# Probabilities times values in a merged attention and expert stage: the values become the stationary operand

## The chip, the cores and the metric

One Trainium2 chip, one of its cores. The metric is the device time of one execution in microseconds, the median of three timed executions. One further execution was recorded by the hardware profiler, and all rows below come from it.

## The reference

A four-layer network on x of 32 batches x 128 rows x 128 columns; every sub-layer is added to x under a tanh gate. The change lies in one of two independent pieces of work which the kernel runs merged in one stage: the third layer's mixture of eight experts, and the fourth layer's attention, cut to this:

```python
x = x + tanh(g_ffn[2]) * L2_ffn(layernorm(x))       # 8 experts, top 2 of 8
# then, a batch of 128 rows at a time, 16 heads of 8 columns:
q, k = split(layernorm(x) @ WqT), split(ctx @ WkT)   # v = split(ctx)
scores = q @ k.T * 8 ** -0.5                         # 16 x 128 x 128
kth    = top_k(scores, 32)[..., -1:]                 # the 32nd largest of each row
p      = softmax(where(scores >= kth, scores, min))
x      = x + tanh(g_xattn[3]) * (p @ v)              # 128 x 128 a batch
```

## The kernel before

One program, written by hand for each engine with semaphores. The stage is `l3_attention`; a tile is one batch (128 rows), and there are 32.

Each engine runs a list of steps in the order in which `schedule` is given them; a pair `(step, behind)` runs `step` for tile `c - behind` in iteration `c`. So iteration c does the query projection and the scores of tile c+1, the row maxima and the cut-offs of tile c, the exponentials and masks of tile c-1, the product with the values for tile c-2, and the division and addition for tile c-3. Experts (`hide`, `gelu`, `output`, `take_y`, `add_experts`) run four tiles ahead in the same lists.

The steps that the change and the prediction touch, for one tile:

- `cutoffs` (VectorE, L2746): 112 instructions, MAX8 and MATCH_REPLACE8, which find the 32nd largest score of each row of each head.
- `negate_max` (GpSimd, L2391) writes `nm` for half of the heads; `exps` n (ScalarE, L2624) then makes the exponentials of heads 4n to 4n+3; `mask` (GpSimd, L2404) zeroes those under the cut-off. For tile 31 the second half is done by VectorE (`negate_last`, `mask_last`).
- `turn_probs` n (TensorE, L2511): four 128x128 transposes into `p_ps`; `take_p` n (ScalarE, L2607) copies these 128x512 into `pT`.
- `apply` n (TensorE, L2518): for each of four heads one matmul with the turned probabilities (128x128) as weights and nine moving columns, the head's eight value columns and a column of ones whose product is the row sum. One matmul in fp32 is two pairs of LDWEIGHTS and MATMUL in the records, so `apply` n is eight pairs.
- `divide` (VectorE, L2766) waits for `av_mm`, the semaphore of the four `apply`, takes the reciprocal of the row sums and multiplies; `add_attention` (GpSimd, L2419) adds to x. `divide` of tile c waits for `x_done` of tile c-1, and `apply` 0 of tile c for `o_ready`, the end of `divide` of tile c-1, since there is one bank `ov_ps`.

On TensorE an iteration is: output 0, hide 0 and 1, output 1, turn_probs 0, turn_rows, hide 2 and 3, apply 0, turn_probs 1, queries, hide 4 and 5, apply 1, turn_probs 2, scores 0, hide 6 and 7, bias_rows, apply 2, turn_probs 3, turn_weights, apply 3, scores 2. Each `apply` n waits for `p_ready` of its `take_p`.

From iteration 32 on, engines that were given `draining` use that list instead. ScalarE's is take_p 0 to 3 (of tile c-2) and then exps 0 to 3 (of tile c-1). VectorE's is divide, negate_last, mask_last; GpSimd's is negate_max 0, mask 0, add_attention. TensorE has none.

After the stage comes a barrier (L2365) and the normalisation `n3f`, whose first instruction is BATCH_NORM_STATS2 at L292.

Of the kernel before, what the change touches and what calls it, by code (L numbers as in the profile page):

```python
# [10 lines left out]
ACT = mybir.ActivationFunctionType  # L11
# [3 lines left out]
P = 128  # L15
# [5 lines left out]
BANK = 512  # L21
# [25 lines left out]
def per_row(ap, n):  # L47

    return ap.unsqueeze(2).to_broadcast([ap.shape[0], ap.shape[1], n])
# [2184 lines left out]
def l3_attention(nc, k):  # L2234
# [4 lines left out]
    H, DA, ROUNDS = 16, 8, 4  # L2239
    Q4, NQ = 4, 4  # L2240
# [3 lines left out]
    AHEAD = 4  # L2244
# [8 lines left out]
    with ExitStack() as ctx:  # L2253
        s = Space(nc, ctx, "l3a", k)
# [2 lines left out]
        w1, w2, b1, bias8, router_bias = wf.w1, wf.w2, wf.b1, wf.bias8, wf.router_bias  # L2257
        two = range(2)
        v_raw = [s.sb(f"v_raw{i}", [P, D]) for i in two]
        v = [s.sb(f"v{i}", [P, H, DA + 1]) for i in range(4)]  # L2260
        qT, kT = s.sb("qT", [P, P]), [s.sb(f"kT{i}", [P, Q4, P]) for i in two]
        score = [s.sb(f"score{i}", [P, H, P]) for i in range(4)]
        work = s.sb("work", [P, H, P])
# [4 lines left out]
        pT = [s.sb(f"pT{i}", [P, Q4, P]) for i in two]  # L2268
# [15 lines left out]
        def spare(tile, start, *shape):  # L2284
            flat = tile[:, :, :].rearrange("p h s -> p (h s)")[:, start:start + int(np.prod(shape))]
            names = "abc"[:len(shape)]
            return flat if len(shape) == 1 else flat.rearrange(f"p ({' '.join(names)}) -> p {' '.join(names)}",
                                                               **dict(zip(names, shape)))
        NE, LQ = NB * E, 2 * NB
        p, rest, eq = (spare(score[3], i * NE, NB, E) for i in range(3))  # L2290
# [8 lines left out]
        ov_ps, p_ps, o2_ps, misc_ps = (s.ps(n, [P, BANK]) for n in ("o", "p", "l2o", "misc"))  # L2299
# [1 line left out]
        h_ps = [s.ps(f"l2h{i}", [P, BANK]) for i in two]  # L2301
        q_ps = s_ps[1][:, 0:P]
        prefix_ps, total_ps, early_ps = p_ps, ov_ps, s_ps[1]
        o_ps = ov_ps[:, 0:H * (DA + 1)].rearrange("p (h d) -> p h d", h=H)
        k_loaded, v_loaded = ([s.sem(f"{n}_loaded{i}") for i in two] for n in "kv")
        (filled, v_ready, q_mm, q_ready, s_mm, s_ready, found, nm_ready, probs_done, compared,
         masked, p_mm, p_ready, av_mm, inv_ready, o_ready, x_done) = (s.sem(n) for n in (
# [11 lines left out]
        def wait(eng, sem, q, per_element, value):  # L2319

            n = q * int(BODY * per_element) + value
            if not isinstance(q, int) or n >= 1:
                eng.wait_ge(sem, n)
# [30 lines left out]
        def in_group(step, at):  # L2354

            return lambda q, u: step(q, u // GT) if u % GT == at else None
# [4 lines left out]
        def for_part(step, n):  # L2361

            return lambda q, c: step(q, c, n)

        with nc.Block() as block:  # L2365
# [17 lines left out]
            def _(pool):  # L2383
# [1 line left out]
                pool.wait_ge(carry_made, 1)  # L2385
                pool.memset(carry[:, :, 0:1], 0.0).then_inc(carry_made, 1)
                for t in v:
                    pool.memset(t[:, :, :], 1.0).then_inc(filled, 1)
                pool.wait_ge(filled, 4)

                def negate_max(q, c, half):  # L2391
# [65 lines left out]
                def norm_scale(q, g):  # L2457
                    n = NORM_STEPS * g

                    def done(i):  # L2460
# [26 lines left out]
                         draining=[(for_part(negate_max, 0), 1), (for_part(mask, 0), 1), (add_attention, 3)])  # L2487

            @block.tensor
            def _(pe):  # L2490
# [27 lines left out]
                def apply(q, c, n):  # L2518
                    wait(pe, p_ready, q, NQ, NQ * c + n + 1)
                    if n == 0:  # L2520
                        wait(pe, v_ready, q, 1, c + 1)
                        wait(pe, o_ready, q, 1, c)
                    for i in range(Q4):
                        h = Q4 * n + i
                        ins = pe.matmul(o_ps[:, h, :], pT[n % 2][:, i, :], v[c % 4][:, h, :], start=True, stop=True)  # L2525
                    ins.then_inc(av_mm, 1)

                def hide(q, u, at):
                    x, i = at // 2, at % 2
                    wait(pe, act_done, q, 2 * EX, 2 * EX * u + at - 1)  # L2530
                    for n in two:
                        ins = pe.matmul(h_ps[i][:, n * WIDE:(n + 1) * WIDE], w1[:, expert(u, x), 2 * i + n, :],  # L2532
                                        k.cols[:, ds(group(q, u) * WIDE, WIDE)], start=True, stop=True)
                    ins.then_inc(h_mm, 1)
# [46 lines left out]
                for at in range(2 * EX):  # L2581
# [9 lines left out]
                              (for_part(scores, 0), -1), (for_part(hide, 6), -AHEAD), (for_part(hide, 7), -AHEAD),  # L2591
                              (in_group(bias_rows, 1), -AHEAD),
                              (for_part(apply, 2), 2), (for_part(turn_probs, 3), 2), (in_group(turn_weights, 0), -AHEAD),
                              (for_part(apply, 3), 2), (for_part(scores, 2), -1)], first=2 - AHEAD)

            @block.scalar
            def _(act):
# [9 lines left out]
                def take_p(q, c, n):  # L2607
                    wait(act, p_mm, q, NQ, NQ * c + n + 1)
                    wait(act, av_mm, q, NQ, NQ * c + n - 1)
                    act.activation(pT[n % 2][:, :, :], p_ps[:, :].rearrange("p (h s) -> p h s", h=Q4), ACT.Copy  # L2610
                                   ).then_inc(p_ready, 1)

                def take_y(q, u, x):
                    wait(act, o_mm, q, PARTS, PARTS * u + x + 1)
                    wait(act, x_added, q, ADDS, ADDS * (u - 1) + 2 * (x + 1))
                    if u % GT == 0:
                        wait(act, w_staged, q, GROUP, u // GT + 1)
                    for n in range(2 * GT):
                        e = expert(u, 2 * x + n // GT)
                        ins = act.activation(y[x][:, n, :], output_bank(u, x)[:, n * D:(n + 1) * D], ACT.Copy,  # L2620
                                             scale=w_stage[u // GT % 2][:, n % GT, e:e + 1])
                    ins.then_inc(y_ready, 1)
# [53 lines left out]
                for u in two:  # L2676
                    for at in range(2 * EX):
# [11 lines left out]
                               (take_queries, -1), (for_part(gelu, 4), -AHEAD), (for_part(gelu, 5), -AHEAD),  # L2689
                               (for_part(take_p, 2), 2), (for_part(take_scores, 0), -1), (for_part(gelu, 6), -AHEAD),  # L2690
                               (for_part(gelu, 7), -AHEAD), (in_group(take_bias, 1), -AHEAD),
                               (for_part(take_p, 3), 2), (in_group(take_weights, 0), -AHEAD), (for_part(take_scores, 2), -1)], first=2 - AHEAD,
                         draining=[*((for_part(take_p, n), 2) for n in range(NQ)), *((for_part(exps, n), 1) for n in range(NQ))])

            @block.vector
            def _(dve):
# [67 lines left out]
                            n += 1  # L2764

                def divide(q, c):  # L2766
                    wait(dve, av_mm, q, NQ, NQ * (c + 1))
                    wait(dve, x_done, q, 1, c)
                    dve.reciprocal(inv[:, :], o_ps[:, :, DA:DA + 1].rearrange("p h o -> p (h o)")).then_inc(inv_ready, 1)
                    wait(dve, inv_ready, q, 1, c + 1)  # L2770
                    dve.tensor_tensor(o_norm[:, :, :], o_ps[:, :, 0:DA], per_row(inv[:, :], DA), ALU.mult
                                      ).then_inc(o_ready, 1)
# [15 lines left out]
                def mask_last(q, c):  # L2788
# [3 lines left out]
                    for h in range(H // 2, H):  # L2792
# [4 lines left out]
                        if h % Q4 == Q4 - 1:  # L2797
# [3 lines left out]
                         draining=[(divide, 3), (negate_last, 1), (mask_last, 2)])  # L2801
# [265 lines left out]
def program(nc, d, out, first=0, last=99):  # L3067

    with ExitStack() as ctx:
# [37 lines left out]
            lambda: l2_cross(nc, k),  # L3107
            lambda: (normalise_measured(nc, k, "n2f", keep_rows=True, gate_w=k.gates_w[:, 2, :], logits=k.logits),
                     l3_attention(nc, k)),
            lambda: l3_block(nc, k),  # L3110
        ]
# [101 lines left out]
```

## Time and profile before

| | us |
|---|---|
| median of three timed executions | 3101.04 |
| lowest and highest of them | 3099.99, 3103.3 |
| the profiled execution's own time | 3106.62 |
| its span, first to last instruction | 3104.8 |
| busy in the span: PE, DVE, ACT, POOL | 2850.7, 2030.3, 1820.0, 1427.0 |

PE is TensorE's matmuls, PEld its weight loads, which overlap them, DVE VectorE, ACT ScalarE, POOL GpSimd. The mean granted clock of TensorE over the span was 0.924 of full speed. The ends of matmuls are modelled, so a distance from start to start says more than a busy time.

### The profile page before, as it was taken

The numbers are of one execution on the slowest core, as the hardware profiler recorded it, in microseconds if no ns is written. First come the engines' busy times: TensorE is split into PE (matmuls) and PEld (weight loads), VectorE is DVE, ScalarE is ACT, GpSimd is POOL, SyncE is SP. The second block draws the span as 40 slices with busy tenths as digits, with TensorE's granted clock in tenths as the row PEclk, the third lists the DMA queues.
The fourth block names the chain that finished last, engine by engine and source line by source line (L and its number), as shares of the span: only waits on it lengthen the run. The fifth ranks groups of instructions, "written<-read, shape, count | busy, mean of one in ns | idle before, by whom it ended". The sixth has DMA issues, their size and how long they took to land. (4 is left out here: it accounts for less than half of the span.)

```text
span 3104.8 us, 70254 instructions
## 1 busy us (share of the span) xinstructions
PE 2850.7 (92%) x21784; PEld 2265.4 (73%) x21784; DVE 2030.3 (65%) x7995; ACT 1820.0 (59%) x5314; POOL 1427.0 (46%) x1744
## 2 busy tenths in 40 slices
PE   7999979987998989999999998999999996597999
PEld 6888854433775778888888777888888874486676
DVE  4444536764653456666666459999999999486433
ACT  5777734443553356666666567788888873353333
POOL 2122117762542434444444248788888876452000
PEclk9999979987998989999999899899999985597999
DMA  3000024433763311111111000000000000001000
GB/s 114 6 5 6 5 53 85 82 82 112 260 235 95 126 49 54 54 54 54 54 54 54 16 10 14 14 13 13 13 13 13 13 14 32 2 18 36 7 10 10
DMA packets 99460, 151.81 MB, mean 49 GB/s; under 512 B 11312, under 2 KB 39488, under 8 KB 98752
## 3 DMA queue, kind: packets, MB, share of 16 engines
q1 hardware_dynamic: 99296, 149.96, 16.5%
q8 instruction: 62, 1.02, 0.1%
q14 instruction: 102, 0.84, 0.1%
HBM read 103.33 MB, written 46.47 MB: 48 GB/s over the span
## 5 line engine op out<-in xcount | busy, mean ns | idle before, releaser
L1899 POOL TENSOR_TENSOR l2a_probs<-l2a_probs,l2a_inv 128x1024 f32<-128x1024 f32 x128 | 242.3, 1893 | 370.5 <-DVE l2a_inv L2065 370.5
L2010 ACT ACTIVATE l2a_probs<-l2a_s_ps,l2a_nm 128x256 f32<-128x256 f32 x512 | 236.1, 472 | 200.0 <-DVE l2a_nm L2041 200.0
L2760 DVE MAX8 l3a_top<-l3a_work 128x8 f32<-128x128 f32 x1536 | 314.1, 276 | 0.0
L2544 PEld LDWEIGHTS l3a_l2o_ps<-net_arena 128*128 128x128 f32 x2016 | 276.6, 222 | 39.0 <-issue 34.9
L2411 POOL TENSOR_SCALAR l3a_above<-l3a_score,l3a_top 128x128 f32<-128x128 f32 x504 | 294.1, 601 | 16.3 <-POOL l3a_probs L2416 7.2
L2544 PE MATMUL l3a_l2o_ps<-net_arena 128*128 128x128 f32 x2016 | 283.4, 308 | 10.6 <-ACT net_l1f_gate L2620 10.6
L2762 DVE MATCH_REPLACE8 l3a_work<-l3a_top,l3a_work 128x128 f32<-128x128 f32 x1024 | 268.8, 274 | 0.0
L2532 PE MATMUL l3a_l2h_ps<-net_cols,net_arena 128*128 (+1 forms) x1024 | 250.9, 388 | 12.9 <-ACT net_arena L2652 11.2
L2532 PEld LDWEIGHTS l3a_l2h_ps<-net_cols,net_arena 128*128 128x128 f32 x1024 | 184.9, 191 | 65.8 <-ACT net_arena L2652 24.5
L721 ACT ACTIVATE l0a_probs<-l0a_score_ps,l0a_nm 128x128 f32<-128x128 f32 x512 | 179.6, 382 | 73.6 <-DVE l0a_nm L770 73.6
L2652 ACT ACTIVATE net_arena<-l3a_l2h_ps,net_l2f_b 128x256 f32<-128x256 f32 x512 | 210.0, 492 | 16.6 <-PE l3a_l2h_ps L2532 13.7
L2525 PEld LDWEIGHTS l3a_o_ps<-l3a_v,l3a_pT 128*128 128x128 f32 x1024 | 148.6, 217 | 73.6 <-ACT l3a_pT L2610 50.2
L755 POOL TENSOR_TENSOR l0a_v<-l0a_v,l0a_inv 128x1024 f32<-128x1024 f32 x32 | 60.9, 1902 | 300.4 <-DVE l0a_inv L794 300.4
L2525 PE MATMUL l3a_o_ps<-l3a_v,l3a_pT 128*128 128x9 f32 x1024 | 148.2, 272 | 49.7 <-ACT l3a_pT L2610 36.5
L2416 POOL TENSOR_TENSOR l3a_probs<-l3a_probs,l3a_above 128x512 f32<-128x512 f32 x126 | 160.2, 1272 | 47.1 <-ACT l3a_probs L2630 37.7
L2041 DVE TENSOR_REDUCE l2a_nm<-l2a_s_ps 128x2 f32<-128x512 f32 x256 | 159.0, 683 | 29.7 <-PE l2a_s_ps L1922 29.6
L2224 DVE SCALAR_TENSOR_TENSOR net_x<-l3f_o_ps,net_weight,net_x 128x128 f32 (+1 forms) x256 | 72.1, 344 | 139.9 <-PE l3f_o_ps L2141 139.5
L770 DVE TENSOR_REDUCE l0a_nm<-l0a_score_ps 128x4 f32<-128x512 f32 x128 | 82.1, 683 | 124.3 <-PE l0a_score_ps L681 124.3
L2630 ACT ACTIVATE l3a_probs<-l3a_score,l3a_nm 128x128 f32<-128x128 f32 x512 | 156.2, 396 | 8.9 <-POOL l3a_nm L2395 8.6
L2176 ACT ACTIVATE l3f_hidden<-l3f_h_ps 128x512 f32<-128x512 f32 x128 | 76.3, 597 | 145.0 <-PE l3f_h_ps L2132 145.0
L1973 PE MATMUL l2a_side_ps<-net_ident,l2a_probs 128*128 128x128 f32 x1024 | 153.4, 280 | 1.0 <-POOL l2a_probs L1899 0.7
L2141 PEld LDWEIGHTS l3f_o_ps<-net_arena,l3f_hidden 128*128 128x128 f32 x1024 | 124.2, 192 | 29.7 <-issue 18.2
(522 smaller groups left out, 7209.1 us busy)
## 6 DMA issues: line engine op xcount, KB each, us to landing
kv_ahead<-l1a_kept SPq DMA_DIRECT2D x128, 256.0 KB, 2.7
l0f_code<-code_rows SPq DMA_DIRECT2D x32, 512.0 KB, 11.5
l2a_kT<-kv_ahead SPq DMA_DIRECT2D x64, 256.0 KB, 2.6
l2a_v<-kv_ahead SPq DMA_DIRECT2D x64, 256.0 KB, 2.6
l1a_shift<-neg_top SPq DMA_DIRECT2D x16, 512.0 KB, 5.0
l1f_chosen<-mask_code SPq DMA_DIRECT2D x64, 128.0 KB, 3.1
keys_ahead<-l1f_keys_kept SPq DMA_DIRECT2D x32, 256.0 KB, 3.3
l3a_kT<-keys_ahead SPq DMA_DIRECT2D x32, 256.0 KB, 2.7
```

Of the source, the lines that this page charges most:

```text
L721: act.activation(probs[c % 2][:, h, :], score[g][:, i * P:(i + 1) * P], ACT.Exp, bias=nm[:, h:h + 1], accum_out=sums[c % 2][:, h:h + 1]).t ...
L1899: pool.tensor_tensor(p[:, :, :], p[:, :, :], per_row(inv[c % 2][a][:, :, :].rearrange("p i o -> p (i o)"), KV), ALU.mult).then_inc(scaled, 1)
L2010: act.activation(probs[c % 2][a][:, 2 * i + odd, :], s_ps[a][odd][:, i * KV:(i + 1) * KV], ACT.Exp, bias=nm[c % 2][a][:, i, odd:odd + 1], ...
L2041: dve.tensor_reduce(nm[c % 2][a][:, :, odd:odd + 1].rearrange("p i o -> p (i o)"), s_ps[a][odd][:, :].rearrange("p (i s) -> p i s", i=2), ...
L2411: ins = pool.tensor_scalar(above[:, i, :], score[c % 4][:, h, :], top[c % 2][:, ROUNDS - 1, h, 7:8], None, ALU.is_ge)
L2416: pool.tensor_tensor(probs[c % 2][:, hs, :], probs[c % 2][:, hs, :], above[:, :, :], ALU.mult).then_inc(masked, 1)
L2525: ins = pe.matmul(o_ps[:, h, :], pT[n % 2][:, i, :], v[c % 4][:, h, :], start=True, stop=True)
L2532: ins = pe.matmul(h_ps[i][:, n * WIDE:(n + 1) * WIDE], w1[:, expert(u, x), 2 * i + n, :], k.cols[:, ds(group(q, u) * WIDE, WIDE)], start=T ...
L2544: ins = pe.matmul(output_bank(u, x)[:, at:at + D], hidden[2 * x + n][:, i, j * P:(j + 1) * P], w2[:, expert(u, 2 * x + n), i, :], start=(i ...
L2652: ins = act.activation(hidden[x][:, 2 * i + n, :], h_ps[i][:, n * WIDE:(n + 1) * WIDE], ACT.Gelu, bias=b1[:, e, 2 * i + n:2 * i + n + 1])
L2760: ins = dve.max(t[:, step // 2, h, :], src)
L2762: ins = dve.match_replace(work[:, h, :], t[:, step // 2, h, :], src, LOWEST)
```

## The change

`apply` swaps the operands. The values of a head, widened from 9 to 32 columns (eight values, a one, 23 zeros), are the weights, and the head's turned probabilities are the 128 moving columns. The product of head 4n+i lands turned, in partitions 32i to 32i+31 of `ov_ps` and columns 128n to 128n+127. A new ScalarE step `take_o` copies the whole bank (128x512) to `oT`, and a new TensorE step `turn_out` makes four 128x128 transposes back into `ov_ps`; `divide` now waits for these. GpSimd fills four wider `v` tiles with zeros and then writes their columns of ones. ScalarE's draining list gets another order.

```diff
-        v = [s.sb(f"v{i}", [P, H, DA + 1]) for i in range(4)]
+        WV = 32
+        v = [s.sb(f"v{i}", [P, H, WV]) for i in range(4)]
+        oT = s.sb("oT", [P, BANK])
...
-        o_ps = ov_ps[:, 0:H * (DA + 1)].rearrange("p (h d) -> p h d", h=H)
+        o_ps = ov_ps[:, :].rearrange("p (h d) -> p h d", h=H)
+        v_blank, o_taken, o_turned = s.sem("v_blank"), s.sem("o_taken"), s.sem("o_turned")
...
                 for t in v:
-                    pool.memset(t[:, :, :], 1.0).then_inc(filled, 1)
+                    pool.memset(t[:, :, :], 0.0).then_inc(v_blank, 1)
+                for i, t in enumerate(v):
+                    pool.wait_ge(v_blank, i + 1)
+                    pool.memset(t[:, :, DA:DA + 1], 1.0).then_inc(filled, 1)
...
                         h = Q4 * n + i
-                        ins = pe.matmul(o_ps[:, h, :], pT[n % 2][:, i, :], v[c % 4][:, h, :], start=True, stop=True)
+                        ins = pe.matmul(ov_ps[WV * i:WV * i + WV, n * P:(n + 1) * P], v[c % 4][:, h, :], pT[n % 2][:, i, :],
+                                        start=True, stop=True)
                     ins.then_inc(av_mm, 1)
+
+                def turn_out(q, c):
+                    wait(pe, o_taken, q, 1, c + 1)
+                    for n in range(NQ):
+                        ins = pe.transpose(ov_ps[:, n * P:(n + 1) * P], oT[:, n * P:(n + 1) * P], k.ident[:, :])
+                    ins.then_inc(o_turned, 1)
...
-                              (for_part(apply, 3), 2), (for_part(scores, 2), -1)], first=2 - AHEAD)
+                              (for_part(apply, 3), 2), (for_part(scores, 2), -1), (turn_out, 2)], first=2 - AHEAD)
...
+                def take_o(q, c):
+                    wait(act, av_mm, q, NQ, NQ * (c + 1))
+                    wait(act, o_turned, q, 1, c)
+                    act.activation(oT[:, :], ov_ps[:, :], ACT.Copy).then_inc(o_taken, 1)
...
-                               (for_part(take_p, 3), 2), (in_group(take_weights, 0), -AHEAD), (for_part(take_scores, 2), -1)], first=2 - AHEAD,
-                         draining=[*((for_part(take_p, n), 2) for n in range(NQ)), *((for_part(exps, n), 1) for n in range(NQ))])
+                               (for_part(take_p, 3), 2), (in_group(take_weights, 0), -AHEAD), (take_o, 2), (for_part(take_scores, 2), -1)], first=2 - AHEAD,
+                         draining=[(for_part(take_p, 0), 2), (for_part(exps, 0), 1), (for_part(exps, 1), 1), (for_part(take_p, 1), 2),
+                                   (for_part(take_p, 2), 2), (for_part(take_p, 3), 2), (take_o, 2), (for_part(exps, 2), 1),
+                                   (for_part(exps, 3), 1)])
...
                 def divide(q, c):
-                    wait(dve, av_mm, q, NQ, NQ * (c + 1))
+                    wait(dve, o_turned, q, 1, c + 1)
```

## Rows read from the trace of the kernel before

**Rows 1.** Busy by window, with instruction counts, granted clock, DMA share and rate.

```profile
core 0: us, PE busy (x) PEld busy (x) DVE busy (x) ACT busy (x) POOL busy (x), PEclk, DMA share, GB/s
...
1975.00:2070.00 95.00, 92.00 (x595) 80.07 (x594) 94.90 (x610) 79.87 (x206) 77.89 (x131) 0.93 0.05 15
...
2638.00:2670.00 32.00, 21.73 (x92) 18.79 (x92) 4.19 (x17) 8.72 (x23) 5.76 (x8) 0.50 0.00 1
```

**Rows 2.** Timeline at tile 11's division: start, length, instruction, idle time before it.

```profile
2176.95 1.06 PE L2525 MATMUL l3a_o_ps<-l3a_v,l3a_pT 128*128 128x9 f32 x8 [0.69 <-ACT l3a_pT L2610]
...
2177.94 1.13 PE L2508 MATMUL l3a_s_ps<-l3a_kT,l3a_qT 32*128 32x512 f32 x4
...
2178.10 0.24 DVE L2769 RECIPROCAL l3a_inv<-l3a_o_ps 128x16 f32<-128x16 f32 x1
...
2179.10 1.08 ACT L2642 ACTIVATE l3a_score<-l3a_s_ps 128x512 f32<-128x512 f32 x2 [2.20 <-PE l3a_s_ps L2508]
```

**Rows 3.** Timeline at tile 0's division.

```profile
1892.44 1.06 PE L2525 MATMUL l3a_o_ps<-l3a_v,l3a_pT 128*128 128x9 f32 x8 [0.47 <-ACT l3a_pT L2610]
...
1896.99 0.23 DVE L2769 RECIPROCAL l3a_inv<-l3a_o_ps 128x16 f32<-128x16 f32 x1
```

**Rows 4.** Busy by window on both sides of the end of one iteration.

```profile
2175.00:2179.00 4.00, 3.31 (x24) 2.29 (x24) 3.97 (x26) 0.90 (x3) 3.05 (x7) 1.00 0.00 0
2179.00:2182.00 3.00, 3.00 (x19) 3.00 (x18) 3.00 (x22) 2.87 (x5) 2.42 (x5) 0.62 0.43 109
```

**Rows 5.** Timeline of TensorE at full clock in this stage, iteration's end.

```profile
2199.57 0.96 PE L2525 MATMUL l3a_o_ps<-l3a_v,l3a_pT 128*128 128x9 f32 x8
2200.38 0.63 PE L2515 MATMUL l3a_p_ps<-net_ident,l3a_probs 128*128 128x128 f32 x4
2200.85 0.38 PE L2553 MATMUL l3a_misc_ps<-net_ident,l3a_l2w_stage 128*8 128x128 f32 x2
```

**Rows 6.** Timeline of TensorE in a later attention stage (weights 128x32).

```profile
2749.72 0.39 PE L2998 MATMUL l3b_s_ps<-net_l3b_proj,l3b_aoT 128*128 128x128 f32 x2
2750.03 0.92 PE L2985 MATMUL l3b_out_ps<-l3b_v,l3b_pT 128*32 128x36 f32 x32
2750.89 0.50 PE L2967 MATMUL l3b_s_ps<-l3b_kT,l3b_qT 32*32 32x128 f32 x32
```

**Rows 7.** Timeline of TensorE in an earlier attention stage (weights 128x64).

```profile
1322.78 1.97 PE L1938 MATMUL l2a_av_ps<-l2a_pT,l2a_v 128*64 128x128 f32 x32
1324.67 0.60 PE L1949 MATMUL l2a_side_ps<-net_cols,net_arena 128*128 x3
```

**Rows 8.** Timeline of the stage's end, tiles 30 and 31.

```profile
2628.87 0.24 POOL L2395 TENSOR_SCALAR l3a_nm<-l3a_top 128x8 f32<-128x8 f32 x1
...
2629.64 0.60 ACT L2610 ACTIVATE l3a_pT<-l3a_p_ps 128x512 f32<-128x512 f32 x1 [2.91 <-PE l3a_p_ps L2515]
...
2638.22 0.24 DVE L2769 RECIPROCAL l3a_inv<-l3a_o_ps 128x16 f32<-128x16 f32 x1
...
2638.93 1.85 PE L2525 MATMUL l3a_o_ps<-l3a_v,l3a_pT 128*128 128x9 f32 x8 [9.33 <-DVE l3a_o_norm L2771]
...
2640.64 1.09 PE L2515 MATMUL l3a_p_ps<-net_ident,l3a_probs 128*128 128x128 f32 x4
2641.77 0.60 ACT L2610 ACTIVATE l3a_pT<-l3a_p_ps 128x512 f32<-128x512 f32 x1 [11.53 <-PE l3a_p_ps L2515]
...
2649.27 4.77 ACT L2630 ACTIVATE l3a_probs<-l3a_score,l3a_nm 128x128 f32<-128x128 f32 x16
...
2656.31 0.26 DVE L2769 RECIPROCAL l3a_inv<-l3a_o_ps 128x16 f32<-128x16 f32 x1 [17.45 <-POOL net_x L2422]
...
2657.04 1.85 PE L2525 MATMUL l3a_o_ps<-l3a_v,l3a_pT 128*128 128x9 f32 x8 [3.92 <-DVE l3a_o_norm L2771]
...
2669.44 0.26 DVE L2769 RECIPROCAL l3a_inv<-l3a_o_ps 128x16 f32<-128x16 f32 x1 [10.26 <-PE l3a_o_ps L2525]
```

**Rows 9.** Two GpSimd lines: durations min/median/max, first and last start.

```profile
L2388 POOL MEMSET l3a_v<- x4: 217/218/218, 1757.0 to 1757.4; 128x144 f32 x4
...
L2401 POOL TENSOR_SCALAR l3a_v<-l3a_v_raw,net_tg x32: 601/618/624, 1806.1 to 2588.0; 128x128 f32<-128x128 f32 x32
```

## The prediction

> **What bounds the kernel now.** I read the page first. TensorE is the busiest engine over the whole span, but the change touches one stage, so its own windows decide. Over 95 us in the middle of the stage VectorE is busy for 94.90 and TensorE for 92.00 [rows 1]. The timeline tells which of the two sets the pace. Tile 0 is divided at 1896.99, tile 11 at 2178.10 and tile 29 at 2638.22 [rows 2, 3, 8]: 25.56 us a tile over the first eleven and 25.56 over all 29, which is VectorE's unbroken row of cut-offs. TensorE is close behind. At tile 0 its last `apply` began 4.55 us before the division, at tile 11 only 1.15 [rows 2, 3]; as that `apply` lasts 1.06, its results were there 0.1 us before VectorE wanted them. TensorE has used up its lead but does not yet hold VectorE back.
>
> Behind tile 29's division VectorE has no cut-offs left, and the order changes: the stage lasts 31.2 us more, until the division of tile 31 at 2669.44, with TensorE at half its clock (0.50, which is 1.2 GHz) [rows 1, 8]. This tail is a chain through TensorE and ScalarE. `apply` 0 of tile 30 starts at 2638.93, released by VectorE. Then for each n comes a cycle: 1.71 us of `apply`, 1.09 of four transposes, 0.60 of `take_p`, and gaps of 0.04 and 0.05, together 3.5 us [rows 8]. The exponentials of tile 31 stand behind all four `take_p` in ScalarE's list and start at 2649.27, though their row maxima, for the first half, were ready at 2629.11 [rows 8]. The mask and the addition follow, so tile 30 is divided only at 2656.31, after 17.45 us of waiting for GpSimd; three more cycles end at 2669.44 [rows 8].
>
> **The change, part by part.**
>
> *The groups of `apply` at full clock.* Eight pairs take 0.81 us from their start to that of the next group [rows 5], and 0.99 in front of the scores [rows 2]; I take 0.85. The new form, 32 columns of weights and 128 moving, is in no row. Its nearest relatives bound it. Weights of 128x32 with 36 moving: 32 instructions in 0.86 us, 27 ns each [rows 6]. Weights of 128x64 with 128 moving: 32 in 1.89 us, 59 ns each [rows 7]; a full-width instruction with 128 moving columns needs about 0.12 (0.47 us for four transposes [rows 5]), so two column halves run side by side. Four quarters should need 27 to 30 ns each, at best 0.22 us a group; without any overlap 8 x 0.112 = 0.9. Entering the form costs a little: two instructions before it take 0.31 us instead of the 0.22 of a steady row [rows 6], so 0.09, and I allow the same for leaving. I take 0.45 us a group, since halves already overlap, and keep 0.4 and 1.1 as ends. Four groups save 4 x 0.40 = 1.6 us of TensorE a tile. The Trainium skill, TensorEngine Tiling, section Key Properties, says that a change of tiling mode drains TensorE; the trace agrees in kind and prices it at that 0.09 us.
>
> *The four transposes of `turn_out`*: 0.47 us at full clock [rows 5], 1.09 at half [rows 8]. Net, TensorE does 1.1 us less a tile.
>
> *`take_o`*: a 128x512 copy like `take_p`, 0.60 us [rows 8]. In the steady part it starts when `apply` 3 ends, about when the scores start at 2177.94. `take_scores`, next behind it in ScalarE's list, waits until 2179.10 anyway, after 2.20 us of idle time [rows 2]: hidden. If TensorE answered that much sooner, it would cost ScalarE 0.6 us of 25.6. `turn_out` sits behind the scores, 1.06 us long, so it finds `oT` ready. What queues behind it is `output` 0, whose turn is 0.5 us later.
>
> *The later signal to `divide`*: it comes behind the scores and transposes, 1.06 + 0.5 + 0.2 us of latency, 1.7 us later than `av_mm`. Taken alone this would make VectorE wait, since it has 0.1 us. But VectorE's pace stays 25.56 while TensorE's falls to about 24.4, so TensorE goes ahead 1.1 us a tile, until ScalarE waits for the row maxima. From a lead of 3.5 us at tile 0 less 1.7, it never touches zero. Steady part: no gain and no loss, the cover being VectorE's cut-offs. Were that cover gone, the gain would be 1.1 us x 29 = 32 us.
>
> *GpSimd's fills*: 128x144 takes 0.22 us [rows 9]; 128x512 is 3.6 times that at most, so 3.2 us for four and under 1 for the small ones, from 1757 on; the first values are written at 1806.1 [rows 9]. Nothing. Writing and reading at a stride of 32 instead of 9 elements: same counts, nothing.
>
> *The tail*, where it counts. At half clock a group's start-to-start time was 1.71, 0.214 a pair [rows 8]. New: 8 x 0.054 for four quarters plus 0.2 for entering and leaving, 0.65. The cycle becomes 3.5 - 1.06 = 2.42. With the new list, ScalarE makes exps 0 and 1 of tile 31 right behind `take_p` 0 of tile 30 at 2630.2, ready by 2633 (0.30 each: 4.77 for 16), under VectorE's cut-offs; the masks of the first half are done before 2638. Now the chain:
> - `apply` 0 of tile 30: 2638.93, not moved. Three cycles: `apply` 3 starts at 2646.2, ends 0.85 later, 2647.05.
> - `take_o` 0.65 with its gap: 2647.7. `turn_out` 1.14: 2648.8. `divide` and multiplication 0.6: 2649.4.
> - exps 2 and 3 behind `take_o`: eight x 0.30, 2650.1. `mask_last` follows head by head, in time for `turn_probs` 2. `take_p` 0 of tile 31: 2650.7.
> - `apply` 0 at 2650.75, three cycles, 2658.0; its end 2658.85; `take_o` 2659.5; `turn_out` 2660.65; `divide` there.
>
> So 2660.65 against 2669.44: 8.8 us. With the overlap of halves only (0.107 a pair), the cycle is 2.83 and the gain 5.4; with none it is 0.2; with free mode changes 10.2. I take 8.8.
>
> Sum: the profiled execution 3106.62 - 8.8 = 3097.8. That execution ran 5.6 above the median; on the median, 3101.04 - 8.8 = 3092.2.
>
> **The rivals.**
>
> 1. *The quarters run one behind another* (the change doesn't do what it says). Each group costs 8 x 0.112 + 0.2 = 1.1 us instead of 0.85; with the transposes TensorE needs 1.5 us more a tile. It already paces VectorE within 0.1 us, so every tile from about the third waits: 27 x 1.5 plus 1.7 for the later signal, less the lead of 3.5, 39 us; the tail gives 0.2. Time 3140. It decides from 0.74 us a group on (0.85 less a quarter of 0.47). For it: no row shows this form. Against: the 59 ns of the halves and the 27 of the quarters. The Trainium skill, TensorE: Matmul & The Clock Gate, Part 3, The mechanism, says that a weight load overlaps a running matmul only if its row group is another; all quarters here use all 128 rows, so by that rule this rival happens. The trace disagrees at 27 and 59 ns. Chance 0.09.
>
> 2. *The clock takes the steady part's slack.* The granted clock is 1.00 from 2175 to 2179, while TensorE has gaps (3.31 busy of 4.00), and 0.62 in the next three microseconds, where it is fully busy [rows 4]: each iteration pays some 1.7 us after its thin end. With less TensorE work the thin stretches grow. A second such fall in each iteration would put TensorE at 24.4 + 1.7 = 26.1 us, 0.5 over VectorE: 14.5 us in 29 tiles, less the lead of 1.8, 13. But it falls only after gaps, and gaps vanish when TensorE is late, so I expect part of it: 0 to 13 us against the tail's 8.8, time 3092 to 3105, most likely 3099. Chance 0.15.
>
> 3. *The tail gains less*, because entering and leaving the form costs more at half clock, or cycles hang on something hidden until now (GpSimd's mask, `mask_last`): 4 to 6 us, 3096. Chance 0.08.
>
> 4. *More*: the clock falls less often, in the tail or behind it, where falls last 3 us and more each: 3084 to 3088. Chance 0.05.
>
> **How the numbers follow.** Forecast 0.63; the rivals 0.09, 0.15, 0.08, 0.05. A measurement of this kernel can tell about 0.2%, 6.2 us: faster ends at 3094.8, slower begins at 3107.2. The forecast's own spread is 3089 to 3096, a little of it inside the bound. Faster: 0.57 of the forecast, 0.02 of rival 2, 0.02 of rival 3, 0.04 of rival 4, 0.65. Slower: rival 1 and 0.05 for the tail of rival 2, 0.14. Same: 0.21. The range 3085 to 3104 holds all but rival 1 and the ends of 2 and 4.
>
> **What would show it.** Right: L2525 as 128*32 with 128 moving, 27 to 40 ns each at full clock; tiles 0 to 29 still 25.56 us apart; tile 29's division at 2638; `turn_out` ending 2 us or more before the division in the steady part; the exponentials of tile 31 starting near 2630; divisions at 2649 and 2660.6. Wrong: DVE L2769 waiting in the middle of the stage for `turn_out` (rivals 1 and 2, told apart by the pace of L2525 and by the granted clock), or cycles above 2.6 us in the tail (rival 3).

## The result, and the profile after

| | before | after |
|---|---|---|
| median of eight timed executions each, us | 3104.94 | 3093.59 |
| lowest and highest | 3099.99, 3110.65 | 3086.55, 3098.28 |
| the profiled execution's own time | 3106.62 | 3095.26 |
| its span | 3104.8 | 3093.5 |
| busy in the span: PE, DVE, ACT | 2850.7, 2030.3, 1820.0 | 2775.3, 2030.8, 1839.8 |
| mean granted clock | 0.924 | 0.934 |

The medians are 11.35 us apart, where 8.8 were forecast. The ratio is 0.9961, 95% interval 0.9947 to 0.9974, which is 8 to 16.5 us. Twice more against the kernel before it came to 0.995 (0.9934 to 0.9967) and 0.996 (0.9946 to 0.9974).

The windows of the changed kernel beside [rows 1], the columns as there:

```profile
1975.00:2070.00 95.00, 86.09 (x615) 66.29 (x615) 94.90 (x606) 81.59 (x205) 77.70 (x129) 0.96 0.04 12
2638.00:2660.00 22.00, 13.14 (x90) 7.26 (x88) 4.35 (x17) 7.59 (x17) 0.94 (x2) 0.50 0.00 1
```

In mid-stage VectorE is as busy as before, 94.90 of 95 us, and still the pace. TensorE issues 20 instructions more and is busy for 5.9 us less, at a clock of 0.96 instead of 0.93. The groups of `apply`, now L2531, at full clock (timeline of TensorE, beside [rows 5]):

```profile
2037.49 0.42 PE L2531 MATMUL l3a_o_ps<-l3a_pT,l3a_v 128*32 128x128 f32 x8
2037.85 0.66 PE L2521 MATMUL l3a_p_ps<-net_ident,l3a_probs 128*128 128x128 f32 x4
```

From the start of a group to that of the next it takes 0.36 us, where the old form had 0.81. The same group through two narrow windows, its first four instructions and its last four:

```profile
2037.49 0.32 PE L2531 MATMUL l3a_o_ps<-l3a_pT,l3a_v 128*32 128x128 f32 x4
2037.63 0.29 PE L2531 MATMUL l3a_o_ps<-l3a_pT,l3a_v 128*32 128x128 f32 x4
```

A single one is recorded with 0.297 us in the first four and 0.272 in the last, so four starts lie within some 0.02 us: about 7 ns from one to the next. Then comes a step of 0.11 us, and the next four again start 7 ns apart. The eight go in two waves of four, one head in each quarter, and the second wave starts 0.13 us after the first. From its last start to the next group pass 0.20 us. A wave by itself costs 0.11 us, so two make 0.22; the other 0.14 of the 0.36 is entering and leaving the form, for which the prediction had allowed 0.18.

The end of the stage (timeline, beside [rows 8]):

```profile
2626.75 2.44 ACT L2648 ACTIVATE l3a_probs<-l3a_score,l3a_nm 128x128 f32<-128x128 f32 x8 [1.73 <-POOL l3a_nm L2401]
...
2635.83 0.24 DVE L2789 RECIPROCAL l3a_inv<-l3a_o_ps 128x16 f32<-128x16 f32 x1
...
2636.55 0.65 PE L2531 MATMUL l3a_o_ps<-l3a_pT,l3a_v 128*32 128x128 f32 x8 [12.17 <-DVE l3a_o_norm L2791]
2637.13 1.12 PE L2521 MATMUL l3a_p_ps<-net_ident,l3a_probs 128*128 128x128 f32 x4
2638.29 0.60 ACT L2623 ACTIVATE l3a_pT<-l3a_p_ps 128x512 f32<-128x512 f32 x1 [9.09 <-PE l3a_p_ps L2521]
2638.93 0.65 PE L2531 MATMUL l3a_o_ps<-l3a_pT,l3a_v 128*32 128x128 f32 x8 [0.69 <-ACT l3a_pT L2623]
...
2643.71 0.65 PE L2531 MATMUL l3a_o_ps<-l3a_pT,l3a_v 128*32 128x128 f32 x8 [0.69 <-ACT l3a_pT L2623]
2644.43 0.60 ACT L2629 ACTIVATE l3a_oT<-l3a_o_ps 128x512 f32<-128x512 f32 x1 [0.77 <-PE l3a_o_ps L2531]
2644.92 2.43 ACT L2648 ACTIVATE l3a_probs<-l3a_score,l3a_nm 128x128 f32<-128x128 f32 x8
2645.08 1.12 PE L2538 MATMUL l3a_o_ps<-net_ident,l3a_oT 128*128 128x128 f32 x4 [0.72 <-ACT l3a_oT L2629]
...
2646.23 0.26 DVE L2789 RECIPROCAL l3a_inv<-l3a_o_ps 128x16 f32<-128x16 f32 x1 [9.75 <-PE l3a_o_ps L2538]
...
2657.57 0.26 DVE L2789 RECIPROCAL l3a_inv<-l3a_o_ps 128x16 f32<-128x16 f32 x1 [8.46 <-PE l3a_o_ps L2538]
```

One cycle is 2638.93 - 2636.55 = 2.38 us (3.5 before). Tile 30 is divided 10.40 us after tile 29 (18.09 before), tile 31 21.74 us after it (31.22 before): the tail is 9.5 us shorter. From tile 0's division (1894.79) to tile 29's 741.0 us pass, as before (741.2), and behind the stage 435.9 (435.4). So in these two executions tiles 0 to 31 give 9.7 of the 11.3 us between the spans; tile 0's division itself comes 2.2 us earlier (1896.99 and 1894.79), and 0.5 is lost again behind the stage. Over the profiled executions below that have VectorE's work unchanged, tile 0's division lies anywhere from 1882 to 1897 us, so from here on the stage is measured from there: "steady" is tile 0's division to tile 29's, "tail" tile 29's to tile 31's, both from the timelines.

### The profile page after: what moved, and what is told of

It reads as the page before. It is cut to its first block and busy times, and to the rows that moved or that the text cites. A ratio compares the mean times of both kernels' runs of the same rounds, so it can differ in the third digit from the quotient of the medians.

```text
span 3093.5 us, 70580 instructions
## 1 busy us (share of the span) xinstructions
PE 2775.3 (90%) x21912; PEld 2135.8 (69%) x21912; DVE 2030.8 (66%) x7995; ACT 1839.8 (59%) x5346; POOL 1428.5 (46%) x1748
## 3 DMA queue, kind: packets, MB, share of 16 engines
q1 hardware_dynamic: 99296, 149.96, 16.5%
## 5 line engine op out<-in xcount | busy, mean ns | idle before, releaser
L2557 PE MATMUL l3a_l2o_ps<-net_arena 128*128 128x128 f32 x2016 | 264.9, 295 | 40.6 <-ACT net_l1f_gate L2638 40.0
L2557 PEld LDWEIGHTS l3a_l2o_ps<-net_arena 128*128 128x128 f32 x2016 | 258.0, 211 | 52.8 <-ACT net_l1f_gate L2638 35.7
L2670 ACT ACTIVATE net_arena<-l3a_l2h_ps,net_l2f_b 128x256 f32<-128x256 f32 x512 | 210.3, 492 | 16.2 <-PE l3a_l2h_ps L2545 14.7
L2054 DVE COPY l2a_pT<-l2a_side_ps 128x512 f32<-128x512 f32 x128 | 88.6, 692 | 77.3 <-PE l2a_side_ps L1973 77.3
L1973 PEld LDWEIGHTS l2a_side_ps<-net_ident,l2a_probs 128*128 128x128 f32 x1024 | 111.8, 141 | 34.8 <-DVE l2a_pT L2054 14.1
## 6 DMA issues: line engine op xcount, KB each, us to landing
l0f_code<-code_rows SPq DMA_DIRECT2D x32, 512.0 KB, 11.3
```

The source lines that it names most:

```text
L1973: ins = pe.transpose(side[j][:, h * P:(h + 1) * P], probs[c % 2][a][:, h, j * P:(j + 1) * P], k.ident[:, :])
L2557: ins = pe.matmul(output_bank(u, x)[:, at:at + D], hidden[2 * x + n][:, i, j * P:(j + 1) * P], w2[:, expert(u, 2 * x + n), i, :], start=(i ...
L2670: ins = act.activation(hidden[x][:, 2 * i + n, :], h_ps[i][:, n * WIDE:(n + 1) * WIDE], ACT.Gelu, bias=b1[:, e, 2 * i + n:2 * i + n + 1])
```

## The experiments

The first theory: the gain is the tail alone, about half of it from the form and half from ScalarE's new order, and the steady part is VectorE's and gives nothing. The rivals: the steady part gives something too, or the clock does.

| kernel | steady, us | tail, us | median | ratio, interval |
|---|---|---|---|---|
| before, profiled | 741.2 | 31.2 | | |
| before, three more profiles | 743.7, 750.0, 744.3 | 31.2 each | 3104.41, 3113.64, 3108.49 (one execution each) | |
| changed | 741.0 | 21.7 | 3093.59 | 0.9961, 0.9947 to 0.9974 |
| changed, again | 741.1 | 21.7 | 3090.30 | 0.9950, 0.9934 to 0.9967 |
| changed, third | 741.1 | 21.7 | 3094.36 | 0.9960, 0.9946 to 0.9974 |
| order alone | 750.0 | 27.1 | 3101.32 | 0.9979, 0.9967 to 0.9991 |
| form alone | 741.1 | 26.5 | 3097.53 | 0.9972, 0.9962 to 0.9983 |
| one quarter | 749.2 | 27.8 | 3108.16 | 1.0004, 0.9991 to 1.0017 |
| before, less VectorE | 741.2 | 32.1 | 3086.45 | 0.9932, 0.9908 to 0.9956 |
| changed, less VectorE | 667.7 | 21.7 | 3007.45 | 0.9686, 0.9656 to 0.9716 |
| warm before the tail | 741.1 | 21.1 | 3091.28 | 0.9954, 0.9936 to 0.9971 |
| two banks | 741.1 | 13.2 | 3085.24 | 0.9934, 0.9920 to 0.9948 |

The first row of the changed kernel is the result above, against 3104.94 us. Each other ratio is against executions of the kernel before in the same series: 3107.36 us for the first four below, 3108.17 for less VectorE and for warm, 3107.12 for two banks and the third run of the changed kernel.

**The changed kernel again.**

> The changed kernel once more, as the yardstick of this call. If the gain comes from the stage's tail, the time from tile 29's division to tile 31's is again 21.8 us (31.2 before) and the total about 9 to 12 us under before.

It came to 0.995, 17.1 us by the medians and so more than the 9 to 12 expected, with steady part and tail as in its first profile.

**The order alone.** The kernel before, but for ScalarE's draining list:

```diff
-                         draining=[*((for_part(take_p, n), 2) for n in range(NQ)), *((for_part(exps, n), 1) for n in range(NQ))])
+                         draining=[(for_part(take_p, 0), 2), (for_part(exps, 0), 1), (for_part(exps, 1), 1), (for_part(take_p, 1), 2),
+                                   (for_part(take_p, 2), 2), (for_part(take_p, 3), 2), (for_part(exps, 2), 1),
+                                   (for_part(exps, 3), 1)])
```

> The kernel before with ScalarE's new draining order alone. Theory: tail divisions hang on the chain through TensorE and on the exponentials; with exps 0 and 1 of tile 31 moved ahead, tile 30 is divided right behind its apply 3 (13.1 us after tile 29 instead of 18.1) and take_p 0 of tile 31 waits for exps 2 and 3, so tile 31 is divided 26.6 us after tile 29 instead of 31.2: 4.6 us gained. Rival, all gain is the new order: 9.5 us gained. Rival, all gain is the new product form: 0.

The tail is 4.1 us shorter (4.6 expected), and tile 30 is divided 13.1 us after tile 29, as expected. Not expected was the steady part, 8.7 us longer than in the profile of before, though no step in it was touched. VectorE's only wait in this kernel between 1900 and 2600 us (who waited for whom: us in total, times, longest), and its window beside [rows 1]:

```profile
DVE l3a_inv L2771 <- PE l3a_o_ps L2525: 8.3, 5, 2.9
```

```profile
1975.00:2070.00 95.00, 91.34 (x552) 77.33 (x552) 90.97 (x579) 73.96 (x188) 74.38 (x127) 0.89 0.04 11
```

The divisions wait five times for the last `apply`; the clock stands at 0.89. That called for more profiles of the kernel before, below.

**The form alone.** The changed kernel with the old order at the end:

```diff
-                         draining=[(for_part(take_p, 0), 2), (for_part(exps, 0), 1), (for_part(exps, 1), 1), (for_part(take_p, 1), 2),
-                                   (for_part(take_p, 2), 2), (for_part(take_p, 3), 2), (take_o, 2), (for_part(exps, 2), 1),
-                                   (for_part(exps, 3), 1)])
+                         draining=[*((for_part(take_p, n), 2) for n in range(NQ)), (take_o, 2),
+                                   *((for_part(exps, n), 1) for n in range(NQ))])
```

> The changed kernel with the old draining order (take_p 0 to 3, take_o, then exps 0 to 3). Theory: cycles of 2.39 us, but the exponentials of tile 31 start only behind take_p 3 or take_o of tile 30, about 9 us after tile 29's division, and mask, addition and division follow 7 us later; tile 31 is divided 26.6 us after tile 29, 4.6 us gained. Rival, all gain is the order: 0 or a loss of 1 to 2 us from take_o and turn_out. Rival, all gain is the form: 9.5 us.

The tail is 4.7 us shorter (4.6 expected). The exponentials of tile 31 again stand behind the whole of tile 30 (a row of its timeline):

```profile
2632.55 4.77 ACT L2648 ACTIVATE l3a_probs<-l3a_score,l3a_nm 128x128 f32<-128x128 f32 x16
```

4.1 and 4.7 make 8.8 of the 9.5 us that both give together. The 0.7 that is left has no run of its own; with the form alone `take_o` of tile 30 stands ahead of these exponentials, too, and that may be it.

In time the form alone gives 9.8 us (interval 5.3 to 11.8) and the order alone 6.0 (2.8 to 10.3). The form's interval lies above the 4.7 us of its tail, so in the timed executions, too, the form gives something beyond the tail.

**All four heads of a group in one quarter.** Same instructions, same work, but the heads that follow one another use the same 32 columns (`divide` reads its bank in the order that this gives; not shown):

```diff
-                        ins = pe.matmul(ov_ps[WV * i:WV * i + WV, n * P:(n + 1) * P], v[c % 4][:, h, :], pT[n % 2][:, i, :],
+                        ins = pe.matmul(ov_ps[WV * n:WV * n + WV, i * P:(i + 1) * P], v[c % 4][:, h, :], pT[n % 2][:, i, :],
```

> The changed kernel, with the four heads of a group all in the same 32-column quarter (group n in quarter n, head i in column block i) instead of one in each; same instructions, same result. Theory, the quarters run side by side: without it a group takes 0.9 to 1.1 us at full clock, 1.7 to 1.9 at half, TensorE again has no slack and VectorE waits for it: 20 to 40 us slower than before, the tail's cycles 3.5 us. Rival, a load of 32 columns alone makes the group short: group 0.5 us or less as in the changed kernel and the time the same as that one's.

This makes rival 1 true. Its timeline and its windows:

```profile
2173.42 1.06 PE L2531 MATMUL l3a_o_ps<-l3a_pT,l3a_v 128*32 128x128 f32 x8
2174.41 0.66 PE L2521 MATMUL l3a_p_ps<-net_ident,l3a_probs 128*128 128x128 f32 x4
```

```profile
1975.00:2070.00 95.00, 89.58 (x590) 70.87 (x589) 94.79 (x605) 80.34 (x204) 77.68 (x130) 1.00 0.04 12
```

(1.06 - 0.27) / 7 = 0.113 us a step, where a whole wave of four costs that in the other layout, and a group is 0.99 us, not 0.36. That the quarters run side by side is hereby shown, and it is what the form's speed is made of. In the tail a cycle is 3.64 us (3.5 expected).

The time was missed: 3108.16 us against 3107.36, no slower, where 20 to 40 us were expected. The steady part grew by 8 us only. Against the old form TensorE has 4 x (0.99 - 0.85) + 0.47 = 1.0 us a tile more to do, which would be 30 us in 29 tiles at the clock of before. But the second row has a granted clock of 1.00, and the next experiment says what that is worth. Once its lead is gone, from tile 9 to tile 25, this kernel takes 26.0 us a tile, 0.4 over VectorE's 25.56.

**The cover removed.** In both kernels VectorE's cut-offs take three rounds of MAX8 instead of four, so they keep the 24 largest scores, not 32; the rest is untouched:

```diff
-    H, DA, ROUNDS = 16, 8, 4
+    H, DA, ROUNDS = 16, 8, 3
```

> The kernel before with three rounds of cut-offs instead of four (the 24 largest scores are kept, not 32), so that VectorE needs about 18.5 us a tile and no longer sets the pace. Theory: TensorE with ScalarE then sets it, at 24 to 25.5 us a tile. Together with its partner (the same cut in the changed kernel) it measures what TensorE's work is worth when nothing covers it: predicted 1.1 us a tile, some 32 us over the stage, plus the tail's 9.5. Rival: the steady part is bound elsewhere (GpSimd, 20.7 us busy a tile, or ScalarE), and the two differ by the tail alone.

> The changed kernel with three rounds of cut-offs instead of four (24 largest scores kept). Theory: 1.1 us a tile less than its partner, 23 to 24.4 us, in total about 40 us less than it. Rival (bound elsewhere): 9.5 us less than it.

The waits of VectorE from 1900 to 2545 us and a window, first of the old form, then of the new one:

```profile
DVE l3a_inv L2769 <- PE l3a_o_ps L2525: 152.3, 25, 10.4
```

```profile
2002.00:2104.00 102.00, 98.95 (x604) 84.03 (x603) 66.97 (x416) 79.29 (x202) 77.92 (x132) 0.88 0.04 13
```

```profile
DVE l3a_inv L2789 <- PE l3a_o_ps L2538: 108.4, 25, 6.5
```

```profile
2002.00:2104.00 102.00, 95.67 (x705) 73.72 (x705) 80.91 (x505) 93.19 (x239) 90.67 (x150) 1.00 0.05 14
```

The steady part of the old form is still 741.2 us, 25.56 a tile, with a quarter of VectorE's rounds gone; the new form does it in 667.7, 23.02 a tile. The kernel as a whole goes from 3108.17 to 3086.45 us with the old form: tile 0 is divided 63.2 us after the first cut-offs instead of 75.5, ahead of the steady part. The two kernels are 79.0 us apart, where about 40 were expected.

That 741.2 is exactly VectorE's figure is chance, because it is an average of three stretches. From the timelines, with the granted clock of TensorE:

| | tiles 0 to 9 | tiles 9 to 25 | tiles 25 to 29 |
|---|---|---|---|
| old form, us a tile (clock) | 26.88 (0.89) | 25.57 (0.93) | 22.5 (0.57) |
| new form, us a tile (clock) | 23.56 (1.00) | 23.76 (1.00) | 18.9 (0.70) |

In the last stretch the experts are done and TensorE has less to do. In the middle one the old form's own pace does equal VectorE's, and in the first it is slower: there was no slack. The new form's margin under VectorE is 1.8 to 2.0 us a tile while the experts run.

Over all 29 tiles the forms differ by 2.5 us a tile, where the prediction had 1.1 (its 32 us, were the cover gone, are 74 in fact). The groups account for some 1.5: four times about 0.85 - 0.36, less 0.47 for the transposes. The other 1.0 is what is left, and by stretches it goes with the clock: the difference is 1.8 us where the old form has 0.93, 3.3 where it has 0.89, and 3.7 in the last stretch, where both are largely at half clock and the groups alone save 4 x (1.71 - 0.59) - 1.09 = 3.4. The one-quarter run fits this. It has 4 x 0.63 us more than the new form, 23.7 + 2.5 = 26.2 us a tile at a clock of 1.00, and measured 26.0. Its 1.0 us more than the old form, at 1.00, puts the old form at about 25.0 to 25.2 us a tile if its clock were 1.00 (an estimate from these runs): under VectorE's 25.56. By this estimate it is the clock that takes the old form's slack.

**Warm into the tail.** 80 transposes of the identity on TensorE, into a bank that nobody reads any more, where the cut-offs of the last tile leave it idle:

```diff
+                def keep_warm(q, c):
+                    if isinstance(q, int) and q * BODY + c == NB - 2:
+                        pe.wait_ge(act_done, 2 * EX * NB)
+                        for n in range(WARM):
+                            pe.transpose(h_ps[0][:, 0:P], k.ident[:, :], k.ident[:, :])
...
-                              (for_part(output, 1), 1 - AHEAD), (for_part(turn_probs, 0), 2),
+                              (for_part(output, 1), 1 - AHEAD), (for_part(turn_probs, 0), 2), (keep_warm, 2),
```

> The changed kernel plus 80 transposes of the identity into an unused bank on TensorE, between turn_probs 0 and apply 0 of tile 30, where TensorE idles for 12 us. Theory: the clock is back at full when the tail's chain starts, a cycle takes about 1.7 us instead of 2.39 and the tail 16 to 17 us instead of 21.7 if the clock holds; if it falls again at once, 20 to 21. Rival: the filler is too long, delays apply 0 and costs 1 to 3 us.

```profile
2626.29 10.63 PE L2545 MATMUL l3a_l2h_ps<-net_ident 128*128 128x128 f32 x80
2638.67 0.43 PE L2531 MATMUL l3a_o_ps<-l3a_pT,l3a_v 128*32 128x128 f32 x8 [1.75 <-DVE l3a_o_norm L2797]
...
2640.37 0.66 PE L2531 MATMUL l3a_o_ps<-l3a_pT,l3a_v 128*32 128x128 f32 x8 [0.69 <-ACT l3a_pT L2629]
```

```profile
2622.00:2630.00 8.00, 6.59 (x38) 5.74 (x37) 8.00 (x52) 2.89 (x7) 7.66 (x13) 0.51 0.00 0
2630.00:2640.00 10.00, 7.94 (x76) 7.29 (x74) 8.57 (x55) 1.63 (x6) 6.53 (x10) 1.00 0.01 2
2641.00:2646.00 5.00, 3.42 (x28) 1.78 (x24) 0.00 (x0) 1.33 (x3) 0.00 (x0) 0.50 0.00 0
```

The clock was 1.00 from 2629.8 on, 3.5 us into the transposes and 8.8 us before the chain, which begins at 2638.67. The chain's first cycle took 1.70 us, the full-clock figure expected; by its second group the clock was 0.50 again (0.66 us for the group instead of 0.43). The tail gains 0.7 us, that one cycle, and ends within the 20 to 21 us expected for a clock that falls at once. Filler this early did not keep the clock in the chain; of the 10 us at 1.00 most passed before it. Transposes that start later were not tried.

**Two banks in the tail.** For the last two tiles the odd groups of turned probabilities go into `h_ps[0]`, free by then, and TensorE gets a list of its own:

```diff
+        def in_tail(q, c):
+            return isinstance(q, int) and q * BODY + c >= NB - 2
+
+        def turned_bank(q, c, n):
+            return h_ps[0] if in_tail(q, c) and n % 2 else p_ps
...
-                    wait(pe, p_ready, q, NQ, NQ * c + n)
+                    wait(pe, p_ready, q, NQ, NQ * c + (max(n - 1, 0) if in_tail(q, c) else n))
+                    if in_tail(q, c):
+                        pe.wait_ge(act_done, 2 * EX * NB)
...
+                         draining=[(for_part(turn_probs, 0), 2), (for_part(turn_probs, 1), 2), (for_part(apply, 0), 2),
+                                   (for_part(turn_probs, 2), 2), (for_part(apply, 1), 2), (for_part(turn_probs, 3), 2),
+                                   (for_part(apply, 2), 2), (for_part(apply, 3), 2), (turn_out, 2)])
```

> The changed kernel, but for the last two tiles the turned probabilities of odd heads go into another PSUM bank, one that is free by then, and TensorE's order in them is turn 0, turn 1, product 0, turn 2, product 1, and so on, so that a turn is no longer held until ScalarE or VectorE has cleared the one bank. My theory, that the tail is a cycle of turn, clearing and product of 2.4 us a head: with two banks two of these cycles overlap, tile 30 follows tile 29's division by about 6.4 us instead of 10.4 and tile 31 by about 14.7 instead of 21.7, some 7 us under the changed kernel on the same chip. The rival: the tail then hangs on the exponentials and the masking of the probabilities, which follow GpSimd's maxima, and gains 2 to 3 us only.

> The changed kernel once more, as the yardstick of the run with two banks: tile 31's division 21.7 us behind tile 29's, 816.5 us from the first cut-offs to tile 29's division, 0.995 to 0.997 of the kernel before.

```profile
2632.34 0.65 PE L2539 MATMUL l3a_o_ps<-l3a_pT,l3a_v 128*32 128x128 f32 x8 [11.31 <-DVE l3a_o_norm L2802]
...
2633.98 0.66 PE L2539 MATMUL l3a_o_ps<-l3a_pT,l3a_v 128*32 128x128 f32 x8
...
2635.61 0.60 PE L2539 MATMUL l3a_o_ps<-l3a_pT,l3a_v 128*32 128x128 f32 x8
2636.36 0.43 PE L2539 MATMUL l3a_o_ps<-l3a_pT,l3a_v 128*32 128x128 f32 x8 [0.16 <-ACT l3a_pT L2634]
```

```profile
2632.00:2636.00 4.00, 3.65 (x32) 2.07 (x32) 0.28 (x2) 0.88 (x2) 0.45 (x1) 0.50 0.00 0
2636.50:2645.00 8.50, 5.21 (x64) 3.20 (x60) 3.04 (x11) 5.68 (x14) 0.49 (x1) 1.00 0.01 3
2646.30:2666.00 19.70, 6.72 (x26) 4.58 (x27) 16.41 (x80) 10.38 (x24) 11.53 (x4) 0.50 0.00 0
```

The timeline shows the first three groups 1.64 us apart with no idle time between, instead of 2.38 with 0.69; tile 30 follows tile 29 after 6.6 us (6.4 expected), tile 31 after 13.2 (14.7). The tail is 8.6 us shorter than the changed kernel's, where 7 were expected. The rest goes with the clock: behind 4 us in which TensorE was busy for 3.65 it was 1.00, from 2636.0 to 2646.3, and the stage ends at 2644.80. In that stretch TensorE was busy for only 5.21 of 8.5 us, a share of 0.61, about that of the changed kernel's tail at 0.50 (13.14 of 22 us, 0.60). So the closed gaps went ahead of the rise, but a busier TensorE is not what held the clock afterwards. As in the run with the transposes it stayed at 1.00 for some 10 us, and here these fell on the chain. In time the kernel is 9.1 us under the changed kernel of the same series, 3085.24 against 3094.36, and the fastest of this study that computes the whole. The third run of the changed kernel came as expected: 21.7 us of tail, 0.996.

**The kernel before, three more profiles.** The first ran after the order alone, the others with the two banks.

> A further look at the kernel before. In its first profile VectorE lost 0.2 us between its first cut-offs and tile 29's division (816.7 us); with the old form and the new draining order it lost 8.9 (825.4). If the old form leaves TensorE no slack, further looks at it scatter between 816.5 and about 825 us; if that one loss came from the order of the list, all stay at 816.7.

> The kernel before, one look. If the old form of the group lacks slack behind VectorE's cut-offs, the stretch from the first cut-offs to tile 29's division is above 816.5 us in some executions (one look so far had 816.7, another 819.2). The rival, that the old form costs nothing there: 816.5 to 817 each time.

> As the look before it: 816.5 to 825 us from the first cut-offs to tile 29's division if slack is lacking, 816.5 to 817 if it is not; the tail 31.2 us in either case.

Windows, one of the first profile of before and two of the second of these, and then a division in the latter (timeline):

```profile
2002.00:2104.00 102.00, 98.32 (x634) 84.88 (x633) 101.86 (x651) 84.19 (x214) 83.75 (x140) 0.94 0.05 13
```

```profile
2002.00:2104.00 102.00, 98.30 (x606) 83.84 (x605) 97.58 (x624) 80.53 (x207) 80.34 (x127) 0.90 0.04 10
...
2206.00:2308.00 102.00, 98.29 (x632) 84.85 (x631) 101.86 (x652) 84.11 (x214) 84.08 (x140) 0.93 0.05 13
```

```profile
2023.00 1.71 PE L2525 MATMUL l3a_o_ps<-l3a_v,l3a_pT 128*128 128x9 f32 x8 [0.69 <-ACT l3a_pT L2610]
...
2024.74 0.26 DVE L2769 RECIPROCAL l3a_inv<-l3a_o_ps 128x16 f32<-128x16 f32 x1 [1.40 <-PE l3a_o_ps L2525]
```

Between 2002 and 2104 us TensorE is busy for 98.3 of 102 us in both, but at 0.94 in one and 0.90 in the other. The last `apply` takes 1.71 us instead of the 1.06 of [rows 2], as the four products lie in a stretch at half clock, and the division waits 1.40 us for it.

From the first cut-offs to tile 29's division the three take 819.2, 825.4 and 819.8 us (816.7 in the first profile, 816.5 in the changed kernel): the theory's scatter, and not the rival's 816.7 each time. So of four profiles of the old kernel the steady part holds 0.2, 2.7, 8.9 and 3.3 us above the changed kernel's 741.05, and 8.9 in the kernel with the order alone; in six profiles with the quarters side by side and all four rounds it holds nothing (741.0 or 741.1 in each). This is a gain in the steady part that the prediction did not see. From the four the mean is 3.8 us.

All of these losses lie in the divisions of tiles 5 to 11. In the first windows of the stage the clock of the old form is 0.88 to 0.93, TensorE's lead runs out, and VectorE waits until the clock is at 0.93 to 0.94. From 2206 us on the four profiles agree: 0.93 to 0.95, and VectorE without a wait.

## Why the prediction was right, and where it was not

- *The sum and its sign* held: 9.5 us in the tail against 8.8. The measured differences, 11 to 17 us, are the tail and about 4 us of waits that the new form no longer has. This second part rests on four profiles of before. In the timed executions the intervals of the form alone (5.3 to 11.8 us, its tail 4.7) and of the second run of the changed kernel (10.3 to 20.5, its tail 9.5) say that there is something beyond the tail; the other two runs of the changed kernel (from 8 us on) could be the tail alone. That the median, 3093.59 us, lies so near the 3092.2 forecast is luck: a larger gain met a kernel before that stood at 3104.94 over eight executions and not at 3101.04.
- *The group at full clock*, taken as 0.45 us between bounds of 0.4 and 1.1, measured 0.36, under the lower bound. Its "at best 0.22", eight times 27 ns, is what two waves take. Entering and leaving cost 0.14, less than the 0.18 allowed, and the margin up to 0.45, "since halves already overlap", was not needed. The one quarter run shows the other end as foreseen (0.99 for the 1.1 of rival 1).
- *The tail's cycle*: 2.42 forecast, 2.38 measured. Tile 30 came 10.40 us after tile 29 (the working gives 10.58), tile 31 21.74 (22.43). The sum was off by 0.7 in all, spread over ends of groups booked at 0.85 that took 0.72, and cycles. The exponentials of tile 31 went ahead as foreseen: ScalarE started them at 2626.75, as soon as their maxima were there.
- *Steady part: no gain and no loss.* Half right. VectorE does set the pace, and the later signal to `divide` cost nothing. But the step "TensorE has used up its lead but does not yet hold VectorE back" was read from one execution at two tiles. With TensorE's own pace 25.57 us in the middle of the stage and 26.9 in its first tiles, against VectorE's 25.56, a longer stretch of low clock goes straight into the stage. The changed kernel has 1.8 to 2.0 us a tile in hand. `turn_out` was to end 2 us or more before the division: in the first profile 3.0 us was the least up to tile 25, in the second 0.9, once.
- *Were that cover gone, 32 us*: 74. The term of 1.1 us a tile was mis-sized twice: 0.4 us a tile is missing for the shorter group (1.5 less 1.1), and 1.0 that goes with the clock.
- *Rival 1*, the quarters one behind another, did not happen: a wave of four costs 0.11 us. The Trainium skill, TensorE: Matmul & The Clock Gate, Part 3, The mechanism, makes the overlap depend on another row group; here all row groups are used by each, and the trace disagrees: four starts 7 ns apart. The rival's price of 39 us was wrong as well: made true, it cost 8 in the steady part. Its work was 1.0 us a tile and not 1.5, and it was priced at the clock of before, where 1.00 was granted.
- *Rival 2*, the clock takes the slack, had the wrong sign. Less work on TensorE did open gaps, but the granted clock went up, from 0.93 to 0.96, and in no profile of the changed kernel did VectorE wait. Its premise that gaps vanish when TensorE is late does not hold for the old form: ahead of the late `apply` at 2023.00 TensorE still had 0.69 us of idle time, and the group fell into half clock.
- *Rival 3*: no cycle above 2.4 us. *Rival 4*, more through the clock: not in the tail, which stayed at 0.50, and not behind it (435.9 us against 435.4). More did come, by some 4 us, in the part that it did not name.

Three things stay open: what about the form moves the granted clock; why the old form's stretch of low clock at the start of the stage ends sooner in one execution than in another; and what moves tile 0's division by up to 15 us between executions.

## What to carry to other kernels

Where two engines are both busy for nearly all of a stage, one profile cannot tell which has slack: take the cover away (here by a shorter loop on VectorE), read the other's pace stretch by stretch and not as one average, and profile the old kernel several times. Products with few columns are cheap with these as weights if each follows one in another quarter of the array's columns: four cost 0.11 us, as much as one. And at the end of a stage, where the pipeline drains, the order in the lists and a second buffer are worth as much as the arithmetic: here 4.1 us for the order and 8.6 for the second buffer with its list (some of it through the clock), beside 4.7 for the form.

## What the hardware showed unexpectedly

- Four matmul instructions with weights of 128x32 and 128 moving columns in fp32, in four different quarters of the columns, start 7 ns apart at full clock, and the next four 0.13 us after the first four. In the same quarter each starts 0.11 us after the one before.
- The granted clock did not follow how busy TensorE is recorded: with nine moving columns it stood at 0.88 while TensorE was busy for 98.95 of 102 us (before, less VectorE), with 128 moving columns at 1.00 while it was busy for 95.67 (changed, less VectorE), and at 1.00, busy for 89.58 of 95, with one quarter. What about the form does this, no run separates.
- 80 transposes brought the clock to 1.00 3.5 us after their start. In that run and in the one with two banks it stayed there for some 10 us, over stretches in which TensorE was busy for 0.79 and for 0.61 of the time, and was 0.50 behind them. What ends such a stretch was not tested.
